# Rotated projections of a decoder layer: the cosine product moves to VectorE, the low part to GpSimd, the query scale into the weights

## What is computed

```python
# cross attention: pairs of neighbours are turned
q = (x @ Wq).reshape(b, n, 32, 16);  k, v = split(ctx @ Wkv)
out = stack([x1 * cos - x2 * sin, x1 * sin + x2 * cos], axis=-1)   # of q and of k
logits = einsum('bqhd,bkhd->bhqk', q, k) * 16 ** -0.5
# second self attention: halves are turned
q, k = h @ wq + bq, h @ wk + bk
q, k = q * cos + rot(q) * sin, k * cos + rot(k) * sin
```

## Time and profile before

| | us |
|---|---|
| runs, median of 3 (lowest, highest) | 2305.2 (2299.11, 2305.41) |
| the profiled execution, its own time | 2297.42 |
| its span, first to last instruction | 2295.6 |
| PE busy | 2069.8 (90%) |
| VectorE (DVE) busy | 1237.3 (54%) |
| ScalarE (ACT) busy | 881.1 (38%) |
| GpSimd (POOL) busy | 708.3 (31%) |
| mean granted TensorE clock | 0.938 of full |

### The profile page before, as it was taken

How to read it: one execution, slowest core, us unless ns; L and a number is a source line. 1 busy time by engine, 2 the same in 40 slices (tenths; PEclk the granted TensorE clock), 3 DMA queues, 4 the chain that set the end, 5 groups by cost and what they waited for, 6 DMA issues and landing times. The chain is left out here.

```text
span 2295.6 us, 31417 instructions
## 1 busy us (share of the span) xinstructions
PE 2069.8 (90%) x10679; PEld 1384.3 (60%) x10679; DVE 1237.3 (54%) x2679; ACT 881.1 (38%) x1662; POOL 708.3 (31%) x610
## 2 busy tenths in 40 slices
PE   6998999887689999996987999979999988999998
PEld 5775666565433434334776666657788877565664
DVE  5446656377689788875976656534313142222221
ACT  3335444343368676773334544433212210111111
POOL 0004555346513232322554654511000000233332
PEclk9997999989789999998997999889999998999999
DMA  5557666345654545443457665453012043433332
GB/s 188 172 192 174 140 136 136 113 163 217 254 127 100 132 116 152 103 124 117 179 192 227 151 152 128 102 200 110 30 63 74 1 172 117 142 60 59 63 65 36
DMA packets 149937, 297.14 MB, mean 129 GB/s; under 512 B 23762, under 2 KB 42324, under 8 KB 148756
## 3 DMA queue, kind: packets, MB, share of 16 engines
q1 hardware_dynamic: 113972, 243.73, 36.6%
q10 hardware_dynamic: 27072, 32.77, 5.3%
q0 software_dynamic: 8736, 18.62, 4.3%
HBM read 181.55 MB, written 102.50 MB: 124 GB/s over the span
## 5 line engine op out<-in xcount | busy, mean ns | idle before, releaser
L1157 ACT ACTIVATE cross_c_prob<-bank 128x512 f32<-128x512 f32 x512 | 271.3, 598 | 124.4 <-PE bank L996 123.4
L1194 DVE TENSOR_REDUCE cross_c_row_max<-bank 128x2 f32<-128x1024 f32 x256 | 300.0, 1212 | 34.8 <-PE bank L965 29.0
L996 PE MATMUL bank<-stack 56*128 56x512 f32 (+4 forms) x768 | 238.7, 437 | 34.1 <-DMA stack<-first_c_max_rows 11.4
L1577 PE MATMUL bank<-moe_hT,moe_w 128*128 128x512 f32 x1056 | 261.5, 405 | 2.2 <-DVE moe_hT L1819 2.2
L965 PE MATMUL bank<-stack 48*128 48x512 f32 (+4 forms) x768 | 218.1, 465 | 36.1 <-PEq L70 19.5
L1577 PEld LDWEIGHTS bank<-moe_hT,moe_w 128*128 128x128 f32 x1056 | 206.5, 197 | 47.3 <-DVE moe_hT L1819 2.6
L996 PEld LDWEIGHTS bank<-stack 56*128 56x128 f32 (+1 forms) x768 | 122.6, 198 | 164.8 <-ACT cross_c_prob L1157 70.3
L1665 PE MATMUL bank<-moe_w_e,moe_hT_e 128*128 x624 | 195.0, 466 | 1.6 <-DMA moe_w_e<-in_experts_packed 1.2
L965 PEld LDWEIGHTS bank<-stack 48*128 48x128 f32 (+1 forms) x768 | 107.4, 206 | 123.6 <-DVE cross_c_row_max L1194 51.7
L1190 DVE CUSTOM_DVE_ANT_0 first_c_masked<-bank,later 128x128 f32<-128x128 f32 (+3 forms) x256 | 115.8, 486 | 88.5 <-PE bank L965 87.6
L1190 DVE CUSTOM_DVE_ANT_0 rotary_c_masked<-bank,later 128x128 f32<-128x128 f32 (+3 forms) x256 | 116.0, 486 | 85.8 <-PE bank L965 84.9
(11 more groups left out here) (344 smaller groups left out, 3967.8 us busy)
## 6 DMA issues: line engine op xcount, KB each, us to landing
moe_w_e<-in_experts_packed SPq DMA_DIRECT2D x8, 2176.0 KB, 9.0
qk_parts<-first_p_parts SPq DMA_DIRECT2D x32, 512.0 KB, 2.7
stack<-qk_parts SPq DMA_DIRECT2D x64, 256.0 KB, 6.9
qk_parts<-cross_p_parts SPq DMA_DIRECT2D x32, 512.0 KB, 2.7
stack<-qk_parts SPq DMA_DIRECT2D x256, 64.0 KB, 2.4
qk_parts<-rotary_p_parts SPq DMA_DIRECT2D x32, 512.0 KB, 2.7
moe_raw<-in_shared_packed SPq DMA_DIRECT2D x11, 768.0 KB, 11.5
stack<-qk_parts SPq DMA_DIRECT2D x16, 512.0 KB, 5.1
```

Source lines behind the costliest of these rows:

```text
L996: last = nc.tensor.matmul(bank[:, 0 : S - q0], k_stack[slot][r : r + ALL_ROWS, at, m * P : (m + 1) * P], q_stack[slot][r : r + ALL_ROWS, a ...
L1157: nc.scalar.activation(probability(g, step // HEADS_AT_ONCE, step % HEADS_AT_ONCE), psum[bank_at["score", n]][:, 0 : S - q0], ACT.Exp).the ...
L1194: nc.vector.tensor_reduce(row_max[:, g % 2, m, j - 1 : j + 1], c.banks[:, first : first + WIDE, :], AX_X, ALU.max).then_inc(s.max_done, 1)
L1577: last = nc.tensor.matmul(psum[bank][:], weights(pa, f, k), hT[p % 2][:, pb, k, :], start=m == 0, stop=m == len(steps) - 1)
```

## The change

In the cross and the rotary projection:

- VectorE makes the cosine product, straight out of the bank, with the bias in the same instruction in the rotary stage (`times_cos`). The bank is free when this is made.
- GpSimd makes the sine product, and then the low part of the tile before. The last low part of a stage stays with VectorE.
- ScalarE's high part follows one tile behind its copy, not two.
- `turned` has three buffers instead of two.
- The query scale goes into the query weights when they are split, not into the copy out of the bank.

```diff
--- before.py
+++ after.py
@@ -246,6 +246,7 @@
     cross, rotary, rope = t.cross, t.rotary, t.rope
     turning = a.kind == "first"
     BODY = a.body
+    TURNED_SLOTS = 3
     ctx = ExitStack()
     with ctx:
         sb = lambda name, shape, dt=F32: ctx.enter_context(nc.sbuf_tensor(f"{a.kind}_p_{name}", shape, dt))
@@ -261,7 +262,7 @@
         v = sb("v", [P, 2, t.v_width])
         parts = sb("parts", [P, 2, 2, S], F32R)
         if rope:
-            straight, swapped, turned = sb("straight", [P, 2, S]), sb("swapped", [P, 2, S]), sb("turned", [P, 2, S])
+            straight, swapped, turned = sb("straight", [P, 2, S]), sb("swapped", [P, 2, S]), sb("turned", [P, TURNED_SLOTS, S])
             cos_t, sin_t = (a.cos_t, a.sin_t) if cross else (sb("cos_t", [P, 1, S]), sb("sin_t", [P, 1, S]))
         stats, mv = sb("stats", [P, TT, 6]), sb("mv", [P, TT, 2])
         std, rstd = sb("std", [P, TT]), sb("rstd", [P, TT])
@@ -289,6 +290,7 @@
         if turning:
             tables = [(freq[:], a.freq), (sign[:], a.sign), (pos[:], a.pos.rearrange("(b t p) d -> p b t d", p=P, t=TT))]
         staged = lambda n: staged_weights(a, n, raw[n % 2])[0]
+        bias_of = lambda what, m: bias_q[:, m : m + 1] if what == "q" else bias_raw[:, 1, m : m + 1]
 
 
 
@@ -311,7 +313,7 @@
 
         freed, count = [], {}
         for bi, what, m in ring:
-            name = {"pos": "pos_sb", "angle": "ang_step", "v": "v_made"}.get(what, "straight_made" if rope else "parts_lo")
+            name = {"pos": "pos_sb", "angle": "ang_step", "v": "v_made"}.get(what, "cos_made" if rope else "parts_lo")
             count[name] = count.get(name, 0) + 1
 
             freed.append(("ang_step", 12 * bi + 1) if what == "angle" else (name, count[name]))
@@ -472,7 +474,7 @@
                         act.wait_ge(s.rotated, n + 1)
                         if n >= 2:
                             act.wait_ge(qk_stored[n % 2], 16 * (qk_before + n // 2))
-                        nc.scalar.activation(parts[:, n % 2, 0], turned[:, n % 2], ACT.Copy).then_inc(s.parts_hi, 1)
+                        nc.scalar.activation(parts[:, n % 2, 0], turned[:, n % TURNED_SLOTS], ACT.Copy).then_inc(s.parts_hi, 1)
 
                     def trig(bi):
                         act.wait_ge(s.ang_step, 12 * (bi + 1))
@@ -484,7 +486,7 @@
                             act.wait_ge(a.carried.raw_here, 16 * (a.after + 1))
                         else:
                             act.wait_ge((s.raw_loaded1, s.raw_loaded0)[n - 1], 16)
-                        nc.scalar.activation(jobs[n][0], staged(n), ACT.Copy).then_inc(s.hi_made, 1)
+                        nc.scalar.activation(jobs[n][0], staged(n), ACT.Copy, scale=t.scale if rope and n == 0 else 1.0).then_inc(s.hi_made, 1)
 
                     wait_for_core(act, a)
                     root(0)
@@ -518,8 +520,8 @@
                                     dst = dst.rearrange("p (h two d) -> p h two d", two=2, d=t.dh)[:, :, 0, :]
                                     src = src.rearrange("p (h d) -> p h d", d=t.dh)
                                 nc.scalar.activation(dst, src, ACT.Copy).then_inc(s.v_made, 1)
-                            if rope and (bi, m) in LAST_VALUES:
-                                high(BODY * n_qk - 2 + LAST_VALUES.index((bi, m)))
+                            if rope and (bi, m) == LAST_VALUES[0]:
+                                high(BODY * n_qk - 1)
                             if m == TT - 1 and turning:
                                 trig(bi)
                             continue
@@ -532,14 +534,12 @@
                             if i >= 2:
 
                                 act.wait_ge(s.swap_made, i - 1)
-                                act.wait_ge(s.cos_made, i - 1)
                             if rotary:
-                                bias = bias_q[:, m : m + 1] if what == "q" else bias_raw[:, 1, m : m + 1]
-                                nc.scalar.activation(straight[:, i % 2], bank[:], ACT.Identity, bias=bias, scale=scale).then_inc(s.straight_made, 1)
+                                nc.scalar.activation(straight[:, i % 2], bank[:], ACT.Identity, bias=bias_of(what, m)).then_inc(s.straight_made, 1)
                             else:
-                                nc.scalar.activation(straight[:, i % 2], bank[:], ACT.Copy, scale=scale).then_inc(s.straight_made, 1)
-                            if i >= 2:
-                                high(i - 2)
+                                nc.scalar.activation(straight[:, i % 2], bank[:], ACT.Copy).then_inc(s.straight_made, 1)
+                            if i >= 1:
+                                high(i - 1)
                         else:
                             if i >= 2:
                                 act.wait_ge(qk_stored[i % 2], 16 * (qk_before + i // 2))
@@ -638,20 +638,36 @@
                             nc.vector.tensor_scalar(x[:], x[:], 3.1415925, -3.1415925, ALU.min, ALU.max).then_inc(s.ang_step, 1)
                             n += 5
 
+                    def times_cos(i, what, m, bank):
+
+                        if i >= TURNED_SLOTS:
+                            dve.wait_ge(s.parts_hi, i - TURNED_SLOTS + 1)
+                            dve.wait_ge(s.parts_lo, i - TURNED_SLOTS + 1)
+                        dst, table = turned[:, i % TURNED_SLOTS], cos_t[:, i // n_qk if cross else 0]
+                        if rotary:
+                            nc.vector.scalar_tensor_tensor(dst, bank[:], bias_of(what, m), table, ALU.add, ALU.mult).then_inc(s.cos_made, 1)
+                        else:
+                            nc.vector.tensor_tensor(dst, bank[:], table, ALU.mult).then_inc(s.cos_made, 1)
+
                     def rotate(i):
 
                         dve.wait_ge(s.cos_made, i + 1)
                         dve.wait_ge(s.sin_made, i + 1)
-                        nc.vector.tensor_tensor(turned[:, i % 2], turned[:, i % 2], swapped[:, i % 2], ALU.add).then_inc(s.rotated, 1)
+                        both = turned[:, i % TURNED_SLOTS]
+                        nc.vector.tensor_tensor(both, both, swapped[:, i % 2], ALU.add).then_inc(s.rotated, 1)
 
                     def low(i):
 
                         dve.wait_ge(s.parts_hi, i + 1)
-                        nc.vector.tensor_tensor(parts[:, i % 2, 1], turned[:, i % 2], parts[:, i % 2, 0].bitcast(F32), ALU.subtract).then_inc(s.parts_lo, 1)
+                        dve.wait_ge(s.parts_lo, i)
+                        nc.vector.tensor_tensor(parts[:, i % 2, 1], turned[:, i % TURNED_SLOTS], parts[:, i % 2, 0].bitcast(F32), ALU.subtract).then_inc(s.parts_lo, 1)
 
                     def weights_low(n):
                         dve.wait_ge(s.hi_made, n + 1)
-                        nc.vector.tensor_tensor(jobs[n][1], staged(n), jobs[n][0].bitcast(F32), ALU.subtract).then_inc(s.lo_made, 1)
+                        if rope and n == 0:
+                            nc.vector.scalar_tensor_tensor(jobs[n][1], staged(n), t.scale, jobs[n][0].bitcast(F32), ALU.mult, ALU.subtract).then_inc(s.lo_made, 1)
+                        else:
+                            nc.vector.tensor_tensor(jobs[n][1], staged(n), jobs[n][0].bitcast(F32), ALU.subtract).then_inc(s.lo_made, 1)
 
                     wait_for_core(dve, a)
                     for part in range(3):
@@ -674,26 +690,25 @@
                         done += 1
                         if what == "v":
                             i = bi * TT + m
-                            if rope and (bi, m) == LAST_VALUES[1]:
+                            if rope and (bi, m) == LAST_VALUES[0]:
                                 rotate(BODY * n_qk - 1)
                             if rotary:
                                 dve.wait_ge(s.proj_done, done)
                                 if i >= 2:
                                     dve.wait_ge(v_stored[i % 2], 16 * (v_before + i // 2))
                                 nc.vector.tensor_tensor(v[:, i % 2], bank[:], bv_row[:], ALU.add).then_inc(s.v_made, 1)
-                            if rope and (bi, m) in LAST_VALUES:
-                                low(BODY * n_qk - 2 + LAST_VALUES.index((bi, m)))
+                            if rope and (bi, m) == LAST_VALUES[1]:
+                                low(BODY * n_qk - 1)
                             continue
                         i = bi * n_qk + 2 * m + (what == "k")
                         if rope:
                             dve.wait_ge(s.straight_made, i + 1)
+                            times_cos(i, what, m, bank)
                             if i >= 2:
                                 dve.wait_ge(s.rotated, i - 1)
 
                             swap = [r ^ 1 for r in range(32)] if cross else [(r + 16) % 32 for r in range(32)]
                             nc.vector.stream_shuffle(swapped[:, i % 2], straight[:, i % 2], swap).then_inc(s.swap_made, 1)
-                            if i >= 2:
-                                low(i - 2)
                             if i >= 1:
```

(9 more changed lines are left out.)

## The result

The changed kernel takes 2319.63 us (median of 4 runs, 2317.95 to 2322.85), the kernel before 2302.15 (4 runs, 2297.03 to 2305.41): 1.0080 of it, 95% interval 1.0054 to 1.0105. It is 17.5 us slower. The forecast was 2315, range 2295 to 2328.

The account below looks back on a forecast made before the run. In the cross stage PE waited mostly for the input's low parts (18.1 us) and ScalarE's bank copy (13.9). Cross +7.9, last cross batch +0.4 and rotary +1.8 gave +10.1 on the median 2305.2: 2315, range 2295 to 2328.

Parts of the forecast that it names:

- signs named beforehand: Profile after: cross PE waits for cosine product 25 us or more, q0 to q1 9 us, three batches 110 to 120.
- One turn: ScalarE and VectorE alternate once a tile, copy to copy 3.1 us; VectorE's cosine product out of the bank takes 0.68.
- A cross batch at full clock: Cross stage, q0's copy to the next batch's, PE at 2.4 GHz: 36.9 us; three batches 110.2 against 109.9.
- The clock: Cross stage: four of twelve q groups behind PE gaps run at the 1.2 GHz level, 1.9 us each, +7.6.
- Last cross batch: Cross stage, batch without norms: 33.0 against 32.6 us, +0.4, with about 3.3 for a store behind ten stack loads.
- Rotary: Rotary stage: batch 39.8 us, three 119.4 (+0.2), two groups at low clock +3.8, last batch -2.2; in all +1.8.
- Exclusion charged at nothing: VectorE's sum, held up by GpSimd's work, could cost 1.0 us more; it falls just after that work, charged 0.
- Weights' low part at full rate: Once per stage, before the first projection: the scalar_tensor_tensor form takes no longer than the plain form's 2.28 us, charged 0.
- Sum: Whole kernel: 7.9 cross, 0.4 last cross batch and 1.8 rotary give +10.1 us, 2315 from the median 2305.2.
- The clock holds: Rival: gaps of 1.7 to 4.2 us leave PE at 2.4 GHz, 7.6 and 3.8 fall out: -1, 2304; chance 0.26.
- the exclusion goes: Rival: GpSimd no longer slows VectorE's norm scaling, 1.75 us twice per rotary batch, 0.8 per cross batch: 2297; chance 0.19.
- Every gap lowers the clock: Rival: eight more q groups at the low clock, 1.9 us each: +25, 2330; chance 0.11.

Follow-up runs that it names:

- the kernel with filled gaps: Changed kernel with 14, 17 and 6 extra unread matmuls on PE ahead of q groups 1, 2 and 3 of each cross batch: 2312.71 us, ratio 1.0057.
- the kernel with both gaps filled: Changed kernel, cross norm parts one and two behind the cosine products, extra matmuls ahead of each next batch's first q group in both stages: 2296.20 us, ratio 0.9979.
- the norm moved: Changed kernel with cross norm parts one and two on VectorE put behind the cosine products of k0 and k1, tuple (1, 3, 4): 2299.96 us, ratio 0.9995.

## Why the prediction was right, and where its sum was off

- **Direction and cause: right.** Slower, in the cross stage, by the late bank and the clock. PE's waits for the product are 41.0 us (25 or more were named), the stall on stores is nearly gone. Two of the signs named beforehand missed, both on the low side: three cross batches were to take 110 to 120 us and took 129.2, and from q0 to q1 9 us, where it was 10.3 to 11.8.
- **One turn, 3.1 us, and the product, 0.68:** 3.11 and 0.69. One assumption in it was off without effect: GpSimd's sine product takes 1.62 and not 1.28, so GpSimd is busy for 2.9 of the 3.1 us.
- **A cross batch at full clock: 36.9 us, three 110.2.** Taking from the measured 129.2 us what each of the twelve groups took over 3.11 us (15.2 in all) leaves 114.0; the kernel with filled gaps gives 116.1 - 1.9 = 114.2 in the same way. So this term was 3.8 us short. The reason is the step from the end of the product to the next q copy: I wrote 2.7 to 2.8, the pitch of back-to-back groups, twelve times; 3.11 is what it takes from a stand. Twelve times 0.36 is 4.3 us, and the other steps and rounding gave 0.5 back. The first matmul behind a gap takes 0.50 (the row at 533.14 above) where the pitch is 0.23.
- **The clock: the mis-sized term.** The prediction took four of the twelve q groups at the low level, 1.9 us each, 7.6. The price was right in the mean (1.45 to 2.47), the count was not: eight of twelve, 15.2. All three q1 and all three q2 groups, behind 2.56 to 4.2 us, were hit, two of three next-q0 groups behind 2.75, and no q3 group behind 1.44. The filled gaps show that these microseconds are the clock's and not a wait's.
- **Last cross batch +0.4:** +1.2. The high part behind the stack loads waited 4.5 us for its store where about 3.3 was counted.
- **Rotary: +1.8 (two clocked groups +3.8, batches 39.8, last batch -2.2).** Measured -0.5. A batch at full clock is 38.9 (the kernel with both gaps filled), 0.9 less than counted: the two scalings of the norm were counted at 3.66 each and took 2.98 and 2.68 in that kernel. The clock took 3.1; the last batch gave -1.1 of the 2.2.
- **Exclusion charged at nothing: held in the changed kernel** (sums 674 ns in the median). But it held by the order of the work, as the kernel before with three buffers shows.
- **Weights' low part at full rate: right.** 2287 ns with the scalar in it, 2.28 us without. The half rate that the Trainium skill (Vector Engine (DVE) Microarchitecture Reference, Points that are easy to get wrong) gives for this form does not show for these float32 tiles.
- **Sum:** +10.1 forecast, +20.0 in the stages of the profiles, +17.5 between the medians. So the sum had half of the loss. That 2315 still came within 4.6 us of 2319.6 is in part luck: the median that it was added to, 2305.2 of three runs, was 3 us above the 2302.2 of four, and the medians differ by 2.5 us less than the stages.
- **Rivals.** "The clock holds" is refuted by the windows above (0.59 and 0.50), and faster, the outcome of "the exclusion goes", by the result. Its mechanism was there on a small scale: the two scalings of a rotary batch took 3.66 and 3.52 us in the kernel before's first batch and 2.98 and 2.68 in the changed kernel's, where the rival had 1.75 less each. "Every gap lowers the clock" had 2330 with twelve groups; eight were hit.

What stays open: what the swap of engines costs or brings by itself at a distance of two tiles, and what decides the clock behind a gap of 2.75 us. The q0 group of the third cross batch took 3.15 us behind such a gap where its neighbours took 4.6 and 4.7; with the norm moved all three were hit; with the other gaps filled one of three was. So the length of the gap alone doesn't decide.

## What to carry to other kernels

When the release of a PSUM bank moves from one engine to another, look at what else stands in the new engine's queue ahead of the releasing instruction, and move that behind it: one tuple was worth the whole loss. Where PE waits between short groups in gaps like the 2.56 to 4.2 us here, price each group behind one at the low clock until the trace says otherwise, and take the group's time from a stand, not from its pitch. Before adding a buffer, ask what its wait was keeping apart: where VectorE has an instruction with two SBUF inputs, look which of the two engines begins first, since the other waits (the sum 1.77 us instead of 0.68, or the sine product 1.62 instead of 1.28).

## What the runs showed of the hardware that was not expected

- In the first three cross batches of the changed kernel the granted clock fell behind gaps of 2.56 to 4.2 us in eight of nine cases and behind none of the three of 1.44 us; extra matmuls in the gap, whose results nobody reads, kept it at 1.00 and took 13 us off three batches.
- A third buffer by itself made the kernel 0.56% slower: the median sum rose from 0.68 to 1.77 us, since GpSimd's sine product had begun before it in most cases.
- A VectorE product with one input in PSUM and one in SBUF took 674 to 692 ns in all 32 cases of the changed kernel, 8 of them with GpSimd at work beside it; with both in SBUF it took 677 to 1777.
- Where a VectorE sum with two SBUF inputs began 0.19 us before GpSimd's sine product, the sum took 0.67 us and the sine product 1.61; where the sine product began 0.5 us before the sum, the sum took 1.78. The one that begins second waits.
- A gap of 2.75 us lowered the clock of the next group in two of three cases in the changed kernel, in three of three with the norm moved, and in one of three with the other gaps filled.
- The time outside the four stretches of the table, nearly all of it code that no kernel here changed, lay between 1996.4 and 2008.4 us from one profiled execution to the next, so a change of 5 us can be read from its stage but not from one span.
